# Two-layer graph attention on one core: packed adjacency words transposed by DMA, tiles of every second row

## The reference

```python
h = jnp.maximum(_layernorm(x, axis=-1), 0.0)
x = x + _L0_gnn_ref(h, adj, L0_gnn_W, L0_gnn_a)
# Wh = h @ W; e = (Wh@a[:256])[:,None] + (Wh@a[256:])[None,:]; masked by adj; softmax; leaky_relu(att @ Wh)
h = jnp.maximum(_layernorm(x, axis=-1), 0.0)
x = x + _L1_gnn_ref(h, adj, L1_gnn_a)
# h1 = h@a[:256]; h2 = h@a[256:]; e = leaky_relu(h1 + h2.T, 0.01); masked by adj > 0; softmax(e) @ h
```

## Time and profile before

| | us |
|---|---|
| three runs | 1840.76, 1846.00, 1846.56; median 1846.0 |
| the profiled execution | 1844.22, its span 1842.1 |
| setup, up to the first aggregation | 0 to 107 |
| layer 0's tile loop | 107 to 1140 |
| layer 1 | 1164 to 1842 |

### The profile page before, as it was taken

How to read it: one execution, slowest core, us unless ns; L and a number is a source line. 1 busy time by engine, 2 the same in 40 slices (tenths; PEclk the granted TensorE clock), 3 DMA queues, 4 the chain that set the end, 5 groups by cost and what they waited for, 6 DMA issues and landing times. The chain is left out here.

```text
span 1842.1 us, 46596 instructions
## 1 busy us (share of the span) xinstructions
PE 1701.4 (92%) x17795; PEld 1460.9 (79%) x17795; DVE 1224.0 (66%) x4738; ACT 940.5 (51%) x1303; POOL 650.3 (35%) x607
## 2 busy tenths in 40 slices
PE   6889999999999999999999997677689999899887
PEld 5648888888888888888888886555578888788776
DVE  6577887888888888875533333677655655555655
ACT  5976554644565555546555541755444444444432
POOL 0000000000000000000255540888877777777775
PEclk9999999999999999999999999888989999999999
DMA  8409877978887797879999981644544444354442
GB/s 301 163 27 383 306 258 272 336 278 298 306 302 274 297 337 270 299 286 357 325 355 361 359 272 53 163 129 134 152 108 128 112 133 107 107 140 112 124 111 86
DMA packets 144110, 410.88 MB, mean 223 GB/s; under 512 B 26193, under 2 KB 92626, under 8 KB 111186
## 3 DMA queue, kind: packets, MB, share of 16 engines
q1 hardware_dynamic: 109714, 329.85, 49.8%
q0 software_dynamic: 27904, 73.43, 14.3%
q10 hardware_dynamic: 6336, 5.77, 1.1%
HBM read 368.94 MB, written 40.03 MB: 222 GB/s over the span
## 5 line engine op out<-in xcount | busy, mean ns | idle before, releaser
L956 PE MATMUL banks<-HV,adjT 128*128 128x257 f16 x8192 | 938.0, 273 | 5.6 <-DVE HV L656 5.2
L956 PEld LDWEIGHTS banks<-HV,adjT 128*128 128x128 fp8e4 x8192 | 788.7, 97 | 138.7 <-DVE HV L656 22.3
L1609 PE MATMUL banks<-Vp,adjp 128*128 128x257 f16 x2560 | 502.3, 278 | 92.7 <-DVE Vn L1409 53.4
L1235 POOL DMA_INDIRECT gat<-h_of_layer,rec x420 | 479.6, 1142 | 127.8 <-issue 125.7
L1609 PE MATMUL banks<-Vn,adjn 128*128 128x257 f16 x2560 | 501.4, 278 | 0.0
L428 ACT ACTIVATE adj_f<-adj_i 128x2048 fp8e4<-128x2048 int32 x256 | 474.1, 1897 | 6.8 <-DMA adj_i<-in_adj 4.5
L1609 PEld LDWEIGHTS banks<-Vp,adjp 128*128 128x128 fp8e4 x2560 | 249.9, 99 | 142.2 <-DVE Vn L1409 57.1
L409 POOL DMA_DIRECT2D HV<-x_after_layer x44 | 25.6, 581 | 849.6 <-DVE rank L879 796.6
L1609 PEld LDWEIGHTS banks<-Vn,adjn 128*128 128x128 fp8e4 x2560 | 252.6, 99 | 41.6
L1271 ACT ACTIVATE adjn<-h1bc,nh 128x512 fp8e5<-128x512 f32 x320 | 208.5, 711 | 104.0 <-PE banks L1609 93.4
L493 ACT ACTIVATE std<-mv,eps 128x1 f32<-128x1 f32 x64 | 18.8, 294 | 306.8 <-DVE mv L688 306.7
(11 more groups left out here) (157 smaller groups left out, 1455.5 us busy)
## 6 DMA issues: line engine op xcount, KB each, us to landing
adj_i<-in_adj SPq DMA_DIRECT2D x256, 1024.0 KB, 7.8
h_of_layer<-hh SPq DMA_DIRECT2D x64, 129.0 KB, 6.0
hs<-h_of_layer SPq DMA_DIRECT2D x64, 129.0 KB, 2.6
xt<-in_x SPq DMA_DIRECT2D x64, 128.0 KB, 6.1
packed_adj<-pk SPq DMA_DIRECT2D x64, 128.0 KB, 6.4
x_after_layer<-x SPq DMA_DIRECT2D x64, 128.0 KB, 6.0
HV<-in_x SPq DMA_DIRECT2D x7, 1024.0 KB, 11.9
gat<-h_of_layer,rec POOLq DMA_INDIRECT x420
```

The lines of the kernel that those rows point to most:

```text
L956: last = nc.tensor.matmul(acc[b][:, 0:DV], adjT_h[:, b, jb, :], V0[:, jb, s, 0:DV], start=(jb == 0 and s == 0), stop=(jb == T - 1 and s == 1))
L1235: pool.indirect_dma_start(gat[:, k % NBUF, s - s0, :], None, h_d, bass.IndirectOffsetOnAxis(ap=rec[:, m, s:s + 1], axis=0))\
L1609: mm = nc.tensor.matmul(bank[2 * i + part][:, 0:DV], m[:, i * P:(i + 1) * P], V[:, j, s, 0:DV], start=(j == 0 and s == 0), stop=(j == T - ...
```

## The change

TensorE no longer packs. VectorE's fold is made for all 64 tiles, and its result, 512 words of 16 bits in each of 128 rows, is transposed by one DMA for each tile, issued by ScalarE (`turn`), into `pk`: four blocks of 128 x 128. A tile is now every second row of 256 consecutive ones, so that two nodes of a pair have bits that are neighbours in a byte pair; bit i of the low byte and of the high byte of a word stand for column tiles that `place` names. An unpack operation now makes one whole row of `adjT` from all 512 words, in place of pieces of eight, and the masks of the two tiles of a pair interleave by bytes, so that the matmuls read their weights at every second byte. The same holds for layer 1, where four operations of 512 elements take the place of eight of 256.

Since the fold must be done and transposed before the unpack, steps reach further ahead: in step t ScalarE converts tile t+3, VectorE folds tile t+2, extracts t+1 and unpacks t+1. x is read in two DMAs for each chunk. In the setup the two first unpacks move behind the reduction of the maximum.

```diff
-    h_by = h_d[1:N + 1, :].rearrange("(a p b) c -> a b p c", a=T // GROUPS, p=P, b=GROUPS)
+    h_by = h_d[1:N + 1, :].rearrange("(q p b) c -> q b p c", q=BQ, p=P, b=BITS)
+
+    def place(t):
+
+        k, q = divmod(t // 2, BQ)
+        return q, (k & 1) * 4 + (k & 2) + k // 4, t % 2
 
     def h_rows(t):
 
-        k = t // (T // GROUPS)
-        return h_by[t % (T // GROUPS), (k & 1) * 4 + (k & 2) + k // 4, :, :]
+        q, i, h = place(t)
+        return h_by[q, i + HALF * h, :, :]
...
+    x_v = x.rearrange("(m p h) d -> p m h d", p=P, h=2)
+    adj_v = adj.rearrange("(m p h) n -> m h p n", p=P, h=2)
+    out_v = out.rearrange("(m p h) d -> p m h d", p=P, h=2)
...
+            adjT = sb("adjT", [P, 2, HALF, BQ * P], u16)
+            adjT_h = adjT[:, :, :, :].bitcast(f8).rearrange("p b i (q r h) -> p b i q r h", q=BQ, h=2)
+            pk = sb("pk", [P, NPK, BQ * P], u16)
...
                 def store_words(t, off, pb):
-                    sp.wait_ge(pk_ready, t + 1)
-                    sp.dma_start(pk_d[bass.ds(t + off, 1), :, :].rearrange("o p n -> p (o n)"),
-                                 pk[:, pb, :]).then_inc(pk_out[pb], 16)
+                    sp.wait_ge(word_in[pb], 16 * (t // NPK + 1))
+                    sp.dma_start(pk_d[t + off, :, :], pk[:, pb, :]).then_inc(pk_out[pb], 16)
...
+
+                def turn(t, b, pb, reuse):
+
+                    act.wait_ge(fold_ready, t * 3 + 3)
+                    if reuse is not None:
+                        act.wait_ge(pk_out[pb], reuse)
+                    act.sem_inc(quarters_seen, 1)
+                    act.dma_start_transpose(pk[:, pb, :].rearrange("p (q r) -> p q r", q=BQ),
+                                            fold1[:, b, 1, :].bitcast(u16)).then_inc(word_in[pb], 16)
+
+                for t in range(2):
+                    turn(t, t, t, None)
                 act.wait_ge(wh_ready, T)
                 act.wait_ge(nM_ready, 1)
...
-                    convert(t + 2, j % 2, range(0, Q // 2), False)
-                    if t_has_tail:
-                        copy_sums(t - 1, (j - 1) % 2)
-                    convert(t + 2, j % 2, range(Q // 2, Q), False)
-                    if t_has_tail:
-                        if reuse is not None:
-                            act.wait_ge(hh_out[(j - 1) % NX], reuse)
-                        finish(t - 1, (j - 1) % NX)
-
-                step(0, 0, None, t_has_tail=False)
+                def step(t, j, reuse, pk_reuse, converts=True, turns=True):
+
+                    if converts:
+                        convert(t + 3, (j + 1) % 2, range(0, Q // 2), False)
+                    copy_sums(t - 1, (j - 1) % 2)
+                    if converts:
+                        convert(t + 3, (j + 1) % 2, range(Q // 2, Q), False)
+                    if reuse is not None:
+                        act.wait_ge(hh_out[(j - 1) % NX], reuse)
+                    finish(t - 1, (j - 1) % NX)
+                    if turns:
+                        turn(t + 2, j % 2, (j + 2) % NPK, pk_reuse)
+
+                convert(2, 0, range(0, Q), False)
+                convert(3, 1, range(0, Q // 2), False)
+                turn(2, 0, 2, None)
+                convert(3, 1, range(Q // 2, Q), False)
                 act.wait_ge(hh_ones, 1)
                 for t in range(1, 2 * NX):
-                    step(t, t % NX, 16 if t > NX else None)
+                    step(t, t % NX, 16 if t > NX else None, 16 * ((t + 2) // NPK) or None)
                 with act.Fori(2, T // NX - 1) as k:
...
-                    four, one = fold4[:, b, :], fold1[:, :, :]
+                    four, one = fold4[:, b, :], fold1[:, b, :, :]
                     if part == 0:
+                        dve.wait_ge(conv_done, t * Q + Q)
...
-                    dve.wait_ge(pack_done, t + 1)
-                    if reuse is not None:
-                        dve.wait_ge(pk_out[pb], reuse)
-                    nc.vector.tensor_copy(pk[:, pb, :], pkps[b][:, :]).then_inc(pk_ready, 1)
-                    if lists:
-                        fold(t, b, 0)
-                    elif lists is False:
-                        dve.sem_inc(adj_read, 1)
-                    dve.wait_ge(pk_ready, t + 1)
-                    words = pk[:, pb, :].rearrange("p (t w) -> p t w", w=WPB)
-                    for k in range(HALF):
-                        dst = adjT[:, b, :, k * WPB:(k + 1) * WPB]
-                        if k <= 6:
-                            i = nc.vector.tensor_scalar(dst, words, PAIR << k, 6 - k, ALU.bitwise_and,
-                                                        ALU.logical_shift_left)
+
+                def make_keys(t, b):
+                    dve.wait_ge(fold_ready, t * 3 + 3)
+                    nc.vector.tensor_tensor(kraw, fold1[:, b, 1, :].bitcast(u16), keypos[:, :], ALU.add)\
+                        .then_inc(keys_ready, 1)
+
+                def unpack(t, b, pb, n_in):
+
+                    dve.wait_ge(word_in[pb], n_in)
+                    for i in range(HALF):
+                        if i <= 6:
+                            last = nc.vector.tensor_scalar(adjT[:, b, i, :], pk[:, pb, :], PAIR << i, 6 - i,
+                                                           ALU.bitwise_and, ALU.logical_shift_left)
                         else:
-                            i = nc.vector.tensor_scalar(dst, words, PAIR << k, k - 6, ALU.bitwise_and,
-                                                        ALU.logical_shift_right)
-                    i.then_inc(adjT_ready, 1)
+                            last = nc.vector.tensor_scalar(adjT[:, b, i, :], pk[:, pb, :], PAIR << i, i - 6,
+                                                           ALU.bitwise_and, ALU.logical_shift_right)
+                    last.then_inc(adjT_ready, 1)
...
                 dve.wait_ge(wh_ready, T)
                 nc.vector.reduce_max(rmax[:, :], scores, AX.X).then_inc(rmax_ready, 1)
                 nc.vector.memset(full[:, :], 0.0)
                 nc.vector.memset(fl[:, :], 0.0)
+                unpack(0, 0, 0, 16)
+                unpack(1, 1, 1, 16)
                 dve.wait_ge(M_ready, 1)
                 nc.vector.tensor_scalar(nM[:, :], Mb[:, :], -1.0, None, ALU.mult).then_inc(nM_ready, 1)
                 dve.wait_ge(p0_ready, 1)
...
+                def step(t, j, n_in, x1_reuse, kept, off, word_n, ahead=True, folds=True, listed=False,
+                         taken=False, e=None):
+
+                    normalise(t - 1, (j - 1) % 2)
+                    if folds:
+                        fold(t + 2, j % 2, 0)
+                    if taken:
+                        extract(t + 1, (j + 1) % UN)
                     if ahead:
-                        take_packed(t + 1, (j + 1) % 2, (j + 1) % NPK, pk_reuse, lists)
-                    if taken:
-                        extract(t, j % UN)
+                        unpack(t + 1, (j + 1) % 2, (j + 1) % NPK, word_n)
                     if e is not None:
-                        decode(e, (j + 1) % UN)
-                    if n_in is not None:
-                        finish(t - 1, (j - 1) % NX, n_in, x1_reuse, kept, off,
-                               (t + 1, (j + 1) % 2) if lists else None)
+                        decode(e, (j + 2) % UN)
+                    finish(t - 1, (j - 1) % NX, n_in, x1_reuse, kept, off,
+                           (t + 2, j % 2) if folds else None, listed)
 
...
-                            last = nc.tensor.matmul(acc[b][:, 0:DV], adjT_h[:, b, jb, :],
+                            q, i, h = place(jb)
+                            last = nc.tensor.matmul(acc[b][:, 0:DV], adjT_h[:, b, i, q, :, h],
                                                     V0[:, jb, s, 0:DV], start=(jb == 0 and s == 0),
                                                     stop=(jb == T - 1 and s == 1))
...
                 with pe.Fori(1, SORT // 2) as k:
                     for b in range(2):
-                        pack(k * 2 + b + 1, (b + 1) % 2, False)
                         aggregate(k * 2 + b, b)
...
-                    words = pkg[:, c // (NC // 2), :, :].rearrange("p g (t w) -> p t g w", w=WPB)
+                    q = c * CB // BITS % (BQ // 2)
+                    words = pkg[:, c // (NC // 2), :, q * P:(q + 1) * P]
+                    for k in range(UB * CB // 2):
+                        i = c * CB % BITS // 2 + k
+                        dst = adjp[:, c // UB % 2, k, :].rearrange("p (g r) -> p g r", g=G)
+                        if i <= 6:
+                            made = nc.vector.tensor_scalar(dst, words, PAIR << i, 6 - i, ALU.bitwise_and,
+                                                           ALU.logical_shift_left)
                         else:
-                            i = nc.vector.tensor_scalar(dst, src, PAIR << k, k - 6, ALU.bitwise_and,
-                                                        ALU.logical_shift_right)
-                    i.then_inc(bits_ready, 1)
```

(20 more changed lines are left out.)

174 lines of the change are left out of this document (59 added, 115 removed).

## The result

The changed kernel takes 2159.0 us (median of 4 runs, 2156.0 to 2161.1) against 1846.3 us before: a ratio of 1.170, 95% interval 1.167 to 1.172. The forecast was 1858 us with 1808 to 1910 us around it. The direction was right; the size, +12 us forecast and +313 us measured, was wrong by a factor of more than twenty.

A forecast was written before the change was run, and what follows sets the result against it. TensorE bound layer 0's list stage, VectorE close behind; afterwards SyncE's order would bind. Terms +24 - 12 + 2 + 0 - 2 = +12 us on 1844.2 us gave 1856 us, 1858 us as median, range 1808 to 1910 us.

The forecast's parts named there:

- What binds before: Layer 0's list stage: TensorE fully busy, could fall to 14.2 us a tile; VectorE close behind, 59.7 us a round after.
- SyncE's loop: List rounds: x read waits for the x1 sum, holding the next adjacency reads; 66.7 us a round, +24 us.
- The words' latency: Landing time L of a tile's DMA transpose, taken as 5 us against 5.3 us of slack, so costing nothing.
- T + 18.8 us: List loop: forecast issue time of a transpose, T being the end of the x1 sum that SyncE's x read awaits.
- rival B: Transposes land late in list rounds: max(31.1, 22.7 + L) + max(35.6, 30.2 + L) us; 1885 to 1929 us, chance 0.12.
- The last 19 tiles: Layer 0's tiles without lists: 12 gain nothing beside GpSimd's reorder, 7 gain 1.7 us each; -12 us.
- Transposes' traffic: 64 transposes of 128 KB on ScalarE's queue, most beside idle DMA time: +2 us.
- Setup: Before the loop: two packs leave, two unpacks move ahead of the negated maximum; taken as 0, maybe -4 to +6 us.
- Layer 1: Fewer, longer unpack operations on VectorE shorten TensorE's 21.0 us wait for masks a little: -2 us.
- Rival A: List rounds: SyncE's loop does not bind, VectorE sets 59.7 us a round; 1796 us, chance 0.30.
- Rival C: Masks at every second byte slow weight loads or ScalarE's signs; 10 ns a matmul would be +133 us; chance 0.04.
- The signs named ahead: List tiles 16.5 to 16.7 us apart; TensorE awaiting masks, converts awaiting reads, VectorE awaiting square root; SyncE's reads in a burst.

The follow-up runs named there:

- first experiment: Changed kernel with masks unpacked from one constant set of words, so VectorE does not wait for transposed words (result wrong): 1868.8 us, ratio 1.014.
- the x read later: Changed kernel with SyncE's x read of a tile put behind the next tile's adjacency reads, result kept: 1806.1 us, ratio 0.982.
- last experiment's third kernel: Kernel before the change with VectorE's loop of list tiles written out, result unchanged: 1842.5 us, ratio 1.000.
- narrow reads: Changed kernel with each adjacency read bringing 64 of 2048 columns from tile 4 on (result wrong): 1749.5 us.
- last experiment: Changed kernel with x read behind the next adjacency reads, unpack behind decoding in bit-decoding steps, and VectorE's list loop written out: 1758.8 us, ratio 0.953.
- the late unpack: Changed kernel with x read behind the next adjacency reads, and unpack behind the decoding in the step that decodes bits: 1788.2 us, ratio 0.971.

## Why the prediction was wrong, by its own steps

- **What binds before.** Right. TensorE's floor of 14.2 us and VectorE's 59.7 us a round were met by the kernels in which nothing else binds (14.3 and 59.4 us), and writing out VectorE's loop did not help the kernel before.
- **SyncE's loop.** Right, to 0.3 us in each of its times (first experiment). Its cost was set at +24 us for 36 tiles; with constant words it is 9 x (69.7 - 63.6) = +55 us, 2.9 us a round of it the dearer way back, which I had carried over from before at 3.0 us. That the kernel without the wait, 1868.8 us, still lies near the forecast of 1858 us is partly luck: its last 19 tiles gain 21 us for 12 us forecast, and what follows the loop 7 us for 2 us, against the dearer rounds. (VectorE's own 27.2 and 32.1 us in the two loops also add up to 59.3 us and not to its 59.7 us, which changes nothing.)
- **The words' latency: the step that failed.** First its size, 5 us for 13.0 us. Of the rows that bounded it (2.3, 6.6, 9.0 us) none had a burst of 4 MB beside it (beside the store of 9.0 us about 2 MB of reads moved before it landed, beside a transpose about 4 MB), and the argument for the low side, "when a turn is issued, the reads before it have landed", does not stand beside the prediction's own rule that a step's sum releases the reads 1.8 us behind it: the transpose hangs on the same sum, through square root and hh, and comes 1 us behind the first read. The prediction timed it by the late root of every second step (T + 18.8 us), and never laid it on one axis with the burst that this step's own sum had released. Even that late transpose is not alone: in the first experiment it goes out at 571.00 us, T + 18.5 us, and the next burst has gone out at 567.65 us, 3.4 us ahead of it.
- **Then its place.** The formula of rival B lets a landing count in two of the four steps of a round. The trace has one transpose in every step, needed in the next: 4 L + 35. At 13 us the formula gives 35.7 + 43.2 = 78.9 us, the trace 88.5 us. At the 5 us of the prediction, the trace's own sum, 4 L + 35, is 55 us, below VectorE's 59.7 us and SyncE's 66.7 us, so the size decides and the place adds to it. Both errors lean the same way.
- **The last 19 tiles.** Forecast -12 us, with nothing gained beside GpSimd's reorder, since the DMA engines were full at 359 GB/s. In the changed kernel they lose 54 us (355.1 us for 300.7 us), with landings up to 16.8 us; with the x read later they gain 34 us (266.3 us), 14.0 us apart. So the full DMA engines before were no limit on them: from 1000 to 1030 us they move 366 GB/s in the kernel before and 397 GB/s with the x read later, at a share of 1.01 and 1.04.
- **Transposes' traffic, setup.** +2 us was not measured alone. Setup: 0, measured +0.7 us, which is within what the kernels with this same setup differ by (first reciprocal at 142.2 to 144.0 us).
- **Layer 1.** Forecast -2 us, measured -8.0 us (2.5 to 12 us less in the ten other kernels with the new layer 1 whose lists are whole). Only the sign is sure, since the old layer 1 takes 708.3 us in the last experiment's third kernel, for 702.2 us. The masks that TensorE waited 21.0 us for the earlier trace rows cost 8.3 us now; the term was sized at a tenth of it, and more than half went:

```profile
PE banks L1599 <- DVE adjp L1438: 8.3, 9, 1.8
```

- **Rival A** (VectorE's own pace) is what the kernel with narrow reads does. **Rival B** is what happened, beyond its bounds and at a chance of 0.12. **Rival C** is out: layer 1's matmuls and weight loads with masks at every second byte take 279 and 99 ns, before 278 and 99 ns. In layer 0 the matmuls' mean is 290 ns for 273 ns, at a granted clock of 0.88 from 400 to 700 us (1.00 before), a mean over stretches at 1.00 (2.4 GHz) and at 0.50 (1.2 GHz, such as 508.6 to 512.0 us); TensorE had idled ahead of each group, and with it busy throughout (last experiment) the clock is 1.00 again and the mean 274 ns. That is a consequence of the wait, and TensorE is no link of the chain 4 L + 35.

The signs named ahead were mixed: TensorE's wait for masks, the burst behind the x read, converts waiting for reads were all seen; the tiles are 22 us apart, not 16.5; VectorE waits for words and hardly for the root.

## What to carry to other kernels

A small DMA that joins a chain (here 128 KB of words, 3.0 us alone) must be priced beside what is in flight at its issue: lay its issue time and the large reads' on one axis, allow for a late start (4.2 us for 1.3 us here), and count the large packets it must take turns with. Before moving work to an earlier step, read each DMA queue for a wait that other transfers stand behind; here one read moved in SyncE's order was worth 353 us and turned a loss of 17% into a gain of 1.8%. And ask in how many steps of a round a latency counts; then look again at waits that were hidden before, such as a loop's way back, once the engine that hid them is faster.

## What the runs showed that I had not expected

- A 128 KB transpose by DMA lands in 2.4 to 3.0 us alone and in 13.0 us beside 4 MB of reads in packets of 8 KB; 11.4, 8.7 and 7.7 us with packets of 4, 2 and 1 KB. Of this 2.9 us is a later first packet, the same with all packet sizes, whose cause stays open; the rest is turns behind read packets.
- VectorE's jump back to the head of its loop costs 3.0 us on quiet DMA engines and 5.6 to 5.8 us on full ones, where the fetched packet of instructions starts some 2.5 us later. Written out, the list loop gives 29 us (1788.2 to 1758.8 us).
- The best of the kernels that keep the result, with the x read later, the late unpack and the loop written out, takes 1758.8 us, 4.7% under the kernel before.
